# Masked attention in a perceiver block: the energies one batch further ahead, and a new order on all engines

## The reference

```python
Q = query @ Wq.T + bq                     # query = layernorm(x), key = value = ctx_1024
K = key @ Wk.T + bk
V = value @ Wv.T + bv
# 16 heads of 16
energy = einsum('bhqd,bhkd->bhqk', Q, K) / sqrt(16)
energy = where(mask == 0, -1e20, energy)
attention = softmax(energy, axis=-1)
x = x + einsum('bhqk,bhkd->bhqd', attention, V).reshape(b, -1, 256) @ Wo.T + bo
```

## Time and profile before

| what | before |
|---|---|
| median of 3 runs | 2080.39 us (2079.14 to 2080.5) |
| span of the profiled execution | 2078.5 us |
| PE busy, PEld busy | 98%, 88% of the span |
| DVE, ACT, POOL busy | 58%, 54%, 24% |
| HBM | 23 GB/s over the span |
| the loop of 32 slots, first E to the last W's end | 1067.5 to 1336.2 us |

### The profile page before, as it was taken

The page is one execution under the profiler, slowest core; times in us unless marked ns, Lnnn a source line. Parts: engine busy times, 40 slices in busy tenths (PEclk is TensorE's granted clock), DMA queues, the critical chain, the costliest instruction groups (busy, mean ns, idle before and its releaser), DMA issues. The chain is left out here.

```text
span 2078.5 us, 46348 instructions
## 1 busy us (share of the span) xinstructions
PE 2031.0 (98%) x18825; PEld 1819.9 (88%) x18825; DVE 1206.5 (58%) x3626; ACT 1123.6 (54%) x2556; POOL 497.8 (24%) x411
## 2 busy tenths in 40 slices
PE   7999999999999999899899999999999999999998
PEld 7999999999999999477768888788999999999998
DVE  6756565656565655567668898735939724233311
ACT  5556565655565656333268777644444444444443
POOL 1000020000000000123311222144444444444444
PEclk9999999999999999999999999999999999999999
DMA  4000200000000000100031110101010101101000
GB/s 152 22 17 22 77 22 17 22 17 22 17 22 16 22 17 2 46 1 1 1 99 33 32 33 23 42 1 34 28 41 1 41 1 41 41 1 41 1 11 31
DMA packets 48786, 57.81 MB, mean 28 GB/s; under 512 B 6528, under 2 KB 40128, under 8 KB 48448
## 3 DMA queue, kind: packets, MB, share of 16 engines
q1 hardware_dynamic: 48576, 54.85, 8.2%
HBM read 46.72 MB, written 2.10 MB: 23 GB/s over the span
## 5 line engine op out<-in xcount | busy, mean ns | idle before, releaser
L963 POOL TENSOR_TENSOR right_h<-right_hr,right_h 128x512 fp32r<-128x512 f32 x256 | 341.3, 1333 | 418.1 <-ACT right_hr L1285 418.1
L1284 ACT ACTIVATE right_h<-bank,dec_b 128x512 fp32r<-128x512 f32 x256 | 176.2, 688 | 390.1 <-PE bank L83 364.3
L83 PE MATMUL bank<-lat_wv,lat_kv_t 128*128 128x256 f32 (+1 forms) x1728 | 259.0, 300 | 0.7 <-issue 0.7
L83 PE MATMUL bank<-lat_kv_t,lat_qk 128*128 128x320 f32 x1536 | 254.7, 315 | 0.0
L83 PEld LDWEIGHTS bank<-lat_kv_t,lat_qk 128*128 128x128 f32 x1536 | 226.3, 188 | 7.7
L2255 ACT ACTIVATE lat_p<-bank,lat_neg_max 128x320 f32<-128x320 f32 x256 | 136.2, 532 | 173.8 <-DVE lat_neg_max L2379 173.8
L83 PEld LDWEIGHTS bank<-lat_wv,lat_kv_t 128*128 128x128 f32 x1728 | 223.0, 190 | 6.8 <-issue 1.1
L83 PE MATMUL bank<-dec_xt,dec_lo 128*128 128x512 f32 x512 | 200.5, 392 | 0.0
L1285 ACT ACTIVATE right_hr<-bank,dec_b 128x512 f32<-128x512 f32 x256 | 174.5, 682 | 0.0
L1768 POOL TENSOR_TENSOR lat_rs_rstdc<-lat_rs_varc,lat_rs_halfc 128x4 f32<-128x4 f32 x16 | 16.2, 1015 | 635.0 <-DVE lat_rs_varc L1760 635.0
L1132 PE MATMUL bank<-dec_hi,right_h 128*128 128x256 f32 x1024 | 161.5, 279 | 1.2 <-POOL right_h L963 1.2
(11 more groups left out here) (327 smaller groups left out, 3914.7 us busy)
## 6 DMA issues: line engine op xcount, KB each, us to landing
raw_w<-in_L_ffn_W SPq DMA_DIRECT2D x16, 1024.0 KB, 6.5
lat_ctx_raw<-in_ctx SPq DMA_DIRECT2D x16, 512.0 KB, 4.1
right_ctx_raw<-in_ctx_turned SPq DMA_DIRECT2D x16, 512.0 KB, 3.7
lat_kv_t<-lat_lt SPq DMA_DIRECT2D x32, 128.0 KB, 2.1
out_x<-x_sb SPq DMA_DIRECT2D x4, 512.0 KB, 2.9
x_sb<-in_x SPq DMA_DIRECT2D x1, 1792.0 KB, 14.6
lat_xl_now<-lat_xl SPq DMA_DIRECT2D x7, 256.0 KB, 4.6
ahead_room<-in_L_xattn_Wq SPq DMA_DIRECT2D x1, 1024.0 KB, 6.9
```

Of the source, the lines that this page charges most:

```text
L83: mm = pe.matmul(out, lhs(a, k), rhs(b, k), start=first and k == 0 and n == 0, stop=last and k == KD - 1 and n == 2)
L963: pool.tensor_tensor(h[:, g % 2, 1, :], hr[:, g % 2, :], h[:, g % 2, 0, :].bitcast(F32), ALU.subtract).then_inc(h_lo, 1)
L1284: act.activation(h[:, n % 2, 0, :], h_bank[n % 2][:, :], ACT.Relu, bias=bias).then_inc(h_hi, 1)
```

## The change

It is an order, on four engines; no piece of work is added or taken away. PE runs K one batch further ahead, K(1) and E(0) before the loop, and its slot becomes W(b-1), E(b+1), side step, K(b+2), T0(b), O, V(b+1), T1(b). T1(b) is thus followed at once by W(b) of the next slot. The side step now stands ahead of T0, and T0's second step (no longer T1's) waits for its readout. ACT's slot becomes weights of m = 0, the side step's readout, one weight of m = 1, K(b+2), one more, copies of T0, the last two weights, copies of T1. DVE's becomes head, residual, normalise(b-1), lowest(b+1) of m = 0, split_keys, early and late side work, lowest(b+1) of m = 1 in two calls, values(b+1). `split_keys` moves from even slots to the odd slot before, on DVE and POOL.

```diff
--- before.py
+++ after.py
@@ -965,9 +965,10 @@
 
             norm_a.power(pool, NCH - 1)
             pool.wait_ge(late_loads, 16 * 20)
+            split_keys(1)
             for b in range(B):
-                if b % 2 == 0 and b // 2 + 1 < NT:
-                    split_keys(b // 2 + 1)
+                if b % 2 == 1 and (b + 3) // 2 < NT:
+                    split_keys((b + 3) // 2)
                 c = b // 8 - 1
                 if b % 8 == 1 and c >= 0:
                     norm_r.power(pool, c)
@@ -1014,8 +1015,12 @@
                 i, half = b // 2, b % 2
                 if i >= 1:
                     pe.wait_ge(c_lo, i)
-                if b >= 1:
-                    pe.wait_ge(v_done, b)
+                if 1 <= b <= 2:
+                    pe.wait_ge(v_done, 1)
+                if b == 2:
+                    pe.wait_ge(k_done, 2)
+                if b >= 3:
+                    pe.wait_ge(v_done, b - 1)
                 for m in range(KD):
                     mm = product3(pe, proj_bank[:, m * S2:(m + 1) * S2], lambda a, kd: wk[:, a, kd, m * P:(m + 1) * P],
                                   lambda a, kd: ctx_t[:, i % 2, a, kd, half * S2:(half + 1) * S2])
@@ -1023,7 +1028,7 @@
 
             def values_proj(b):
                 i, half = b // 2, b % 2
-                pe.wait_ge(k_done, b + 1)
+                pe.wait_ge(k_done, min(b + 2, B) if b else 1)
                 for t in range(2):
                     at = half * S2 + t * P
                     mm = product3(pe, proj_bank[:, t * D:(t + 1) * D], lambda a, kd: ctx_t[:, i % 2, a, kd, at:at + P],
@@ -1046,7 +1051,7 @@
                     pe.wait_ge(p_ready, 8 * b + 4 * m + 2 * half + 2)
                     if 2 * b + m >= 1:
                         pe.wait_ge(pt_done, 2 * (2 * b + m) - 1 + half)
-                    if m == 1 and half == 1 and b in in_slot:
+                    if m == 0 and half == 1 and b in in_slot:
                         pe.wait_ge(*read_out(*in_slot[b]))
                     for n in range(2):
                         for t in range(2):
@@ -1170,26 +1175,28 @@
             pe.wait_ge(q_dve, NCH)
             pe.wait_ge(b_cols, 1)
             pe.wait_ge(loads, 96)
+            keys_proj(1)
+            energies(0)
             for b in range(B):
-                energies(b)
-                if b >= 1:
-                    turn(b - 1, 1)
-                if b + 1 < B:
-                    keys_proj(b + 1)
                 if b >= 1:
                     weigh(b - 1, 0)
                     weigh(b - 1, 1)
+                if b + 1 < B:
+                    energies(b + 1)
+                if b in in_slot:
+                    pe.wait_ge(pt_done, 4 * b)
+                    side_step(*in_slot[b])
+                if b + 2 < B:
+                    keys_proj(b + 2)
                 turn(b, 0)
+                if b >= 2 and b % 2 == 0:
+                    project_output(b // 2 - 1)
                 if b + 1 < B:
                     values_proj(b + 1)
-                if b in in_slot:
-                    pe.wait_ge(pt_done, 4 * b + 2)
-                    side_step(*in_slot[b])
-                if b >= 2 and b % 2 == 0:
-                    project_output(b // 2 - 1)
-            pe.wait_ge(s_low, 8 * B)
-            hidden(0, 0)
-            turn(B - 1, 1)
+                if b == B - 1:
+                    pe.wait_ge(s_low, 8 * B)
+                    hidden(0, 0)
+                turn(b, 1)
             weigh(B - 1, 0)
             weigh(B - 1, 1)
             for n in range(1, E * STEPS):
@@ -1305,30 +1312,28 @@
             act.wait_ge(side_psum, 1)
             act.copy(b1[:, :], banks[7][:, 0:E * NF]).then_inc(b_cols, 1)
             act.copy(wrs[:, :, 0], wr[:, :, :]).then_inc(wr_split, 1)
+            keys_proj(1)
             for b in range(B):
                 if b == 4:
                     act.wait_ge(r_const, 4)
-                weights_of(b, 0, 0)
-                if b >= 1:
-                    turn(b - 1, 1)
-                for r in range(1, R):
+                for r in range(R):
                     weights_of(b, 0, r)
-                if b + 1 < B:
-                    keys_proj(b + 1)
+                if b in in_slot:
+                    side_read(*in_slot[b])
+                weights_of(b, 1, 0)
+                if b + 2 < B:
+                    keys_proj(b + 2)
+                weights_of(b, 1, 1)
                 turn(b, 0)
-                for r in range(R):
+                for r in range(2, R):
                     weights_of(b, 1, r)
-                if b == B - 1:
-                    side_read(*in_slot[b])
+                turn(b, 1)
                 if b % 8 == 7 and b >= 15:
                     cell_exps(b // 8 - 1)
                 if b % 8 == 0 and b >= 16:
                     cell_tanh(b // 8 - 2)
                 if b in (17, 18):
                     expert0_high(b - 17)
-                if b in in_slot and b < B - 1:
-                    side_read(*in_slot[b])
-            turn(B - 1, 1)
             for n in range(E * STEPS):
                 e = n // STEPS
                 relu(e, n % STEPS)
@@ -1593,22 +1598,27 @@
                 dve.wait_ge(wr_split, 1)
                 dve.tensor_tensor(wrs[:, :, 1], wr[:, :, :], wrs[:, :, 0].bitcast(F32), ALU.subtract).then_inc(wr_split, 1)
 
+            split_keys(1)
+            lowest(0, 0, 0, R)
+            lowest(0, 1, 0, R)
             for b in range(B):
                 slot_head(b)
                 if b >= 3 and b % 2 == 1:
                     residual(b // 2 - 1)
-                lowest(b, 0, 0, R)
-                lowest(b, 1, 0, R)
-                if b % 2 == 0 and b // 2 + 1 < NT:
-                    split_keys(b // 2 + 1)
+                if b >= 1:
+                    normalise(b - 1)
+                if b + 1 < B:
+                    lowest(b + 1, 0, 0, R)
+                if b % 2 == 1 and (b + 3) // 2 < NT:
+                    split_keys((b + 3) // 2)
                 if b % 2 == 1:
                     add_bias(b // 2)
-                if b >= 1:
-                    normalise(b - 1)
                 slot_early(b)
+                slot_late(b)
                 if b + 1 < B:
+                    lowest(b + 1, 1, 0, 2)
+                    lowest(b + 1, 1, 2, R)
                     values_proj(b + 1)
-                slot_late(b)
                 if b == 2:
                     late_constants()
```

## The result

| | before | after |
|---|---|---|
| median | 2080.44 us | 2134.41 us (2132.75 to 2135.57, 4 runs) |
| ratio to before, 95% interval | | 1.026 (1.0248 to 1.0272) |
| span of the profiled execution | 2078.5 us | 2131.0 us |
| first piece of the loop's stretch to the next layer | 268.7 us | 323.2 us |

The change makes the kernel 54 us slower; the forecast was 37 us, and the measured time lies just outside its range. The direction and the place were right; the size was not, and one move that the forecast had at nothing cost a large part of what is missing. The whole loss lies in the loop: up to its start, and from its end on, the two traces differ by about 1 us.

A forecast was written before the change was run, and what follows sets the result against it. PE was taken to bound the loop. Terms 7.5 + 15 + 18 + 5 = 45.5 us, less 9 of old waits, gave +36.5 on the 2078.5 span, 2115; the median lies 1.9 above: 2117 us, range 2104 to 2130.

The forecast's parts named there:

- T1 directly ahead of W: Even slots, PE: W waits for ACT's copy, which K no longer covers; 0.5 us in each of 15 slots, 7.5 us.
- The residual in odd slots: Odd slots: W waits 0.75 us for DVE's residual, T1's second step 0.1; +1.0 us in each of 15 slots, 15 us.
- A light pair: An odd and an even slot in slots 1 to 10: forecast at 8.0 and 8.4 us, 16.4 together.
- The side readouts: Heavy slots: T0's second step waits for DVE's reading of the side step, late in DVE's list; 18 us, between 0 and 25.
- Costless moves: Split of keys one slot earlier on DVE and POOL, expert 1's load sooner: no cost, POOL's 2.57 us ending before K needs them.
- The clock: Rival: PE's clock falls after waits in about eight slots, 1.7 us each, 14 us in all, 2131 us; chance 0.10.
- Start and end: Loop's ends: E(1) waits for the eight lowest, last slot loses cover, slot 30 has no K (0.9); together +5 us.
- only the copy is late: Rival: readouts and residual come in time, only ACT's copy delays W; +9 us, 2090 us; chance 0.13.
- does what it says: Rival: energies a batch ahead remove every wait inside the slots; 9 us won, 2071 us, down to 2066; chance 0.04.
- nothing to be measured: Rival: copy costs 13 us, 9 are won, the start is hidden by the queries' end; 2076 to 2084 us; chance 0.05.
- A reading: Profile of the loop before the change: ACT and DVE were said to have a fifth of their time or less to spare.

## Why the prediction was wrong, point by point

- **T1 directly ahead of W**: right, and priced too high. W takes 1.33 to 1.38 instead of 1.03 in every slot where nothing else is later: 0.30 to 0.35, not 0.45 to 0.5. The 0.43 was read off, where T1's second step itself takes 0.56 (1334.85 - 1334.29) and not 0.42; W alone lost 0.30 there as well. That the old order would have paid it twice I had not seen.
- **The residual in odd slots**: right chain, a term too small. 1.28 instead of 0.75, because the chain is 2.0 and not 1.8, and because PE is through with T1 0.68 behind the last weight's end and not 1.1. Of these 0.42 some 0.2 are O, which takes 0.68 and not 0.95 when V follows it (V then takes 1.62 and not 1.54); the rest was not followed further. T1 loses 0.36 in odd slots, where ACT's weights and copies are late, and not 0.1.
- **A light pair** came close, 16.73 against 16.4, with some luck: reckoned from T1's end, as the forecast was, an even slot takes 7.97 and not 8.4, an odd one 8.77 and not 8.0, and the two errors nearly cancel.
- **The side readouts**: right slots, right releasers. T0's excess over 0.85 is 22.0 in the eight slots 17, 18, 21, 23 to 26 and 29, where the forecast's 18 holds 14.9 for them (2.8 more are for W in slots 17 and 25, and 0.3 for slot 13). With POOL's split later they hold 14.7. Slot 18 (3.3 against 1.8) has ACT's cast ahead of DVE's list, which the forecast had nowhere.
- **"Costless moves"**: the step that failed. I asked of the split only whether POOL's 2.57 would end before K needs them, and they do: K never waited for it. I did not ask beside what they would run. Moved to the odd slots they meet `cell_weights`, the norm's closings and an expert's low part, ahead of the readout on which T0 depends and of the lowest on which E depends. Undone by itself it is 12.8 us, the largest piece that no term or rival held.
- **The clock**: the rival was named, with its place (T0's waits, eight slots) and 14 us; it came in four of these slots (18, 21, 23, 25) and in slot 31, with 10, and 7.6 came back when PE was kept at work. The error was to set it against the forecast as another case with a chance of 0.10, where it follows from the waits that the forecast itself held. Which waits bring it no row here foretells. Even one and the same wait, the 3.07 us between E(0) and E(1), left the clock at 1.00 in the profile after and brought it to 0.50 in that of the kernel with POOL's split later, where first piece to W(0) takes 14.4 us instead of 12.3; so the start's 3.0 is a lucky reading.
- **Start and end**: 4 forecast (the 5 less the 0.9 of slot 30), 5.4 measured. **Other rivals**: "only the copy is late" fell with the residual and the readouts; "does what it says" and "nothing to be measured" fell with all of them.
- **A reading**: ACT has a quarter of its time to spare in the heavy stretch (154.45 of 205 us), not a fifth; nothing in the sum hangs on it.

The missing 18 us are, in the rows, 0.37 in each of 15 pairs (5.5, an estimate from the light ones), 5.7 in the readouts (7.1 more in T0, 1.4 less in W and in slot 13), about 4.6 in the V and O that ran at the lower clock in slots 18, 21, 23 and 25 (V 2.46, 2.26, 2.66 and 2.71 instead of 1.54), 3.8 in E's waits for the lowest, which I had at nothing (slots 10, 16, 20 and 28 lose 0.5 to 1.3 each), 0.9 in slot 19 and 1.5 at both ends. That is 22; against it stand waits that came shorter than in a light pair (in slots 19 and 27 the one for the residual, 0.7 each), and the rest of the difference was not followed. By the kernel with POOL's split later, E's waits and most of the readouts' 5.7 are POOL's. The pieces that the experiments took away overlap: POOL's 12.8 and the clock's 7.6 are not to be added, since a shorter wait can also keep the clock. How much of POOL's 12.8 is clock was not tried.

## What to carry to other kernels

An operation moved on a helping engine has two prices: whether it is ready in time, and what it runs beside (here 0.38 us on VectorE became 1.49). The second is read by laying its new place over the other engine's list; here that list ended in a readout for which TensorE waited, and with POOL's start moved behind it the kernel was 12.8 us faster. The same holds for work that did not move: ACT's cast stayed where it was, and the new order put DVE's list behind it.

When a forecast holds waits of some microseconds in TensorE's list, a fall of the clock behind some of them belongs into the sum, with a chance for each, and not among the rivals: here it came behind 2.23 us and did not behind 3.27. And an order that puts a producer next to its consumer should be priced on every engine between them: a gap of 0.35 on PE became 0.92 through ACT in one order, and 12 us of loss through DVE in another that closed the gap.

## What the runs showed of the hardware

- A VectorE addition or subtraction of two tiles in SBUF, 128x256, takes 0.38 to 0.42 us alone and 1.47 to 1.49 beside GpSimd's 128x512 subtraction; on 4 columns 0.15 to 0.17 alone and up to 1.25. That both sizes end 0.01 to 0.28 behind the end of GpSimd's instruction fits standing still until then, and not running slower. GpSimd can lose too: 3.61 instead of 2.57 for its two, beside one of 128x1024 on VectorE, which took 2.31 instead of 1.54.
- 112 matmuls that feed nothing made the kernel 7.6 us faster, with the clock at 0.99 instead of 0.97; the four slots where the clock had fallen are 7.3 us shorter.
- The same four matmuls of O take 0.95 to the next piece ahead of E and 0.68 ahead of V; V then takes 1.62 instead of 1.54, so 0.19 of the 0.27 is left.
